# Attention values and output projection of a vision tower: Wv and Wo multiplied into one matrix, or applied one after the other

## The reference, cut to what matters

```python
# _L0_ffn_ref: x is (64, 170, 128); 2 heads of 64
hx = _layernorm(x, ln_g, ln_b)
q = (hx @ Wq).reshape(b, n, h, dh).transpose(0, 2, 1, 3)
k = (hx @ Wk).reshape(b, n, h, dh).transpose(0, 2, 1, 3)
v = (hx @ Wv).reshape(b, n, h, dh).transpose(0, 2, 1, 3)
...                                  # q, k normalised, causal scores, softmax
o = jnp.einsum('bhqk,bhkd->bhqd', attn, v)
y = o.transpose(0, 2, 1, 3).reshape(b, n, d) @ Wo
gate = jax.nn.softmax(y @ gate_W + gate_b, axis=-1)
hid = jax.nn.gelu(jnp.einsum('bnd,edf->bnef', y, W1) + b1)   # 8 experts, all of them
eo = jnp.einsum('bnef,efd->bned', hid, W2) + b2
out = jnp.einsum('bned,bne->bnd', eo, gate)
```

## Time and profile before

| | us |
|---|---|
| time, median of 3 (1700.39 to 1704.64) | 1700.49 |
| the profiled execution's own time | 1700.59 |
| its span, first to last instruction | 1698.5 |
| TensorE busy | 1569.1 |
| VectorE busy | 1304.2 |
| ScalarE busy | 1090.9 |
| GpSimd busy | 370.5 |

### The profile page before, as it was taken

One profiled execution on the slowest core, in us unless ns is written; L12 is line 12 of the kernel. 1 busy time (PEld: TensorE's weight loads), 2 busy tenths in 40 slices (PEclk: granted clock), 3 DMA queues, 4 the chain that ended last, 5 costly groups with the idle time before them and its releaser, 6 DMA issues.

```text
span 1698.5 us, 31246 instructions
## 1 busy us (share of the span) xinstructions
PE 1569.1 (92%) x10875; PEld 1105.7 (65%) x10875; DVE 1304.2 (77%) x2462; ACT 1090.9 (64%) x1833; POOL 370.5 (22%) x213
## 2 busy tenths in 40 slices
PE   6984599999999999999999999999999999999988
PEld 3542476667676676666676767666676767677665
DVE  7993378696878778796878777786968787777766
ACT  2321267676776767676767767676767677676766
POOL 5456002021211202020212112020202121120313
PEclk8996599999998989899999989899999999898979
DMA  4311010010101010100101010102001010101020
GB/s 179 130 44 72 0 67 1 26 49 8 66 8 66 8 66 0 74 0 19 55 8 66 8 66 8 66 0 74 0 15 60 8 66 8 66 8 67 1 75 9
DMA packets 14255, 68.88 MB, mean 41 GB/s; under 512 B 1808, under 2 KB 1808, under 8 KB 11664
## 3 DMA queue, kind: packets, MB, share of 16 engines
q1 hardware_dynamic: 13936, 67.71, 11.0%
q10 hardware_dynamic: 288, 0.77, 0.1%
HBM read 62.56 MB, written 5.92 MB: 40 GB/s over the span
## 4 chain that ended last, share of the span: by engine, by line
PE 79%; DVE 13%; issue 4%; ACT 3%; DMA 0%; POOL 0%; DVEq 0%; POOLq 0%; ACTq 0%
PE pair L864 23%; PE pair L881 23%; PE pair L667 8%; PE pair L808 4%; PE pair L653 4%; PE pair L679 2%; PE pair L751 2%; PE pair L766 2%; PE pair L695 2%; DVE root_t L1051 2%; PE pair L781 2%; PE pair L796 2%; DVE area L1131 2%; DVE root_t L1053 1%; PE pair L848 1%
## 5 line engine op out<-in xcount | busy, mean ns | idle before, releaser
L1208 DVE TENSOR_TENSOR area<-area 128x680 f16<-128x680 f32 x512 | 529.2, 1038 | 89.3 <-ACT area L566 80.5
L561 ACT ACTIVATE area<-pair,pack_b_sb 128x680 f32<-128x680 f32 x512 | 425.9, 832 | 237.8 <-PE pair L864 235.3
L864 PE MATMUL pair<-area,ws 128*128 128x340 f16 x3072 | 562.7, 322 | 0.2 <-ACT area L566 0.2
L881 PE MATMUL pair<-area,ws 128*128 128x340 f16 x3072 | 534.0, 310 | 13.0 <-DVE area L1220 12.3
L864 PEld LDWEIGHTS pair<-area,ws 128*128 128x128 f16 x3072 | 310.4, 102 | 162.6 <-ACT area L566 3.6
L881 PEld LDWEIGHTS pair<-area,ws 128*128 128x128 f16 x3072 | 296.8, 98 | 160.3 <-DVE area L1220 20.3
L399 POOL TENSOR_TENSOR area<-area 128x680 f32<-128x680 f32 x112 | 215.7, 1926 | 642.9 <-DVE area L1220 642.9
L566 ACT ACTIVATE area<-pair,pack_b_sb 128x680 f16<-128x680 f32 x384 | 317.8, 828 | 0.0
L1220 DVE SCALAR_TENSOR_TENSOR area<-pair,pack_b_sb,area 128x340 f32<-128x340 f32 x256 | 134.4, 565 | 40.9 <-PE pair L881 40.9
L396 POOL TENSOR_TENSOR area<-area,ht 128x680 f32<-128x680 f32 x16 | 33.7, 2107 | 589.9 <-DVE area L1220 589.9
L531 ACT ACTIVATE area<-pair,nbias,root 85x85 f32<-85x85 f32 (+1 forms) x256 | 112.3, 463 | 17.3 <-DVE nbias L1119 17.3
(11 more groups left out here) (180 smaller groups left out, 1780.9 us busy)
## 6 DMA issues: line engine op xcount, KB each, us to landing
area<-gate_scratch SPq DMA_DIRECT2D x16, 1360.0 KB, 9.9
area<-gate_scratch SPq DMA_DIRECT2D x16, 1020.0 KB, 7.1
area<-cells SPq DMA_DIRECT2D x14, 448.0 KB, 3.5
area<-gate_scratch SPq DMA_DIRECT2D x16, 340.0 KB, 4.4
tower_out<-area SPq DMA_DIRECT2D x16, 340.0 KB, 2.3
area<-cells SPq DMA_DIRECT2D x13, 416.0 KB, 4.1
area<-w SPq DMA_DIRECT2D x1, 2048.0 KB, 9.9
pack_b_sb<-pack_b SPq DMA_DIRECT2D x1, 1044.0 KB, 9.8
```

The lines of the kernel that those rows point to most:

```text
L561: nc.scalar.activation(two(hid[slot % NHID]), halves(hid_ps[slot % 2]), ACT.Gelu_apprx_tanh, bias=col(COL_B1 + slot)).then_inc(hid_ready, 1)
L864: last = mm(hid_ps[slot % 2][:, j, 0:TH], lhs[:, w], rhs[:, j * TH:(j + 1) * TH], start=(i == 0), stop=(i == 2))
L881: last = mm(eo_ps[:, j, 0:TH], lhs[:, w], rhs[:, j * TH:(j + 1) * TH], start=(m % CH == 0 and i == 0), stop=(m % CH == CH - 1 and i == 2))
L1208: v.tensor_tensor(hl[slot % NPART], hid[slot % NHID], hh[slot % NPART], ALU.subtract).then_inc(hlo_ready, 1)
```

## The change

Wv and Wo are not multiplied with each other any more.
- Preparation: the products and copies for `wvo` are gone. VectorE splits `wv` (128 x 128) into `wv_h`, `wv_l`. The bias column comes from one product with `wv`.
- `values`: the moving operand is `wv_h` or `wv_l` with 128 columns; `values_evac` copies 256 columns an image in place of 512.
- `weigh`: the weights of a head are its 85 x 64 values, and the result goes to its 64 partitions of PSUM (and of the array's columns), so the heads no longer add up into the same place.
- New on ScalarE: `o_evac(j)` copies half j of the weighted values, with the bias, to `o32` (in the place of `qs`). New on TensorE: `project(j)`, one f32 product of `wo` with that half, 340 columns, into `hid_ps[1]`. `y_evac(j)` now waits for it, and copies from there without a bias.
- Order: TensorE has `project(0)` between `weigh(2)` and `weigh(3)`, `project(1)` between `var2` and the logits. ScalarE has `o_evac(0)`, `y_evac(0)`, sq2, `o_evac(1)`, `y_evac(1)`, the variance's evacuation. VectorE has dev2 ahead of `y_parts(0)`.

```diff
-        wqk_h, wqk_l, wvo_h, wvo_l = (sb(n, [128, 2 * D], F16) for n in ("wqk_h", "wqk_l", "wvo_h", "wvo_l"))
+        wqk_h, wqk_l = (sb(n, [128, 2 * D], F16) for n in ("wqk_h", "wqk_l"))
+        wv_h, wv_l = (sb(n, [128, D], F16) for n in ("wv_h", "wv_l"))
...
-                nc.scalar.activation(vp[:, b * 512:(b + 1) * 512], hid_ps[b // 2][0:QC, b % 2, :],
+                nc.scalar.activation(vp[:, b * 2 * D:(b + 1) * 2 * D], hid_ps[b // 2][0:QC, b % 2, 0:2 * D],
                                      ACT.Copy).then_inc(vp_ready, 1)
...
+            def o_evac(g, j):
+
+                act.wait_ge(pv_ps, NB * g + 2 * (j + 1))
+                nc.scalar.activation(o32[:, j * TH:(j + 1) * TH], hid_ps[0][:, j, 0:TH], ACT.Identity,
+                                     bias=att_b[:, 2:3]).then_inc(o_ready, 1)
+
             def y_evac(g, j):
 
-                act.wait_ge(pv_ps, NB * g + 2 * (j + 1))
-                nc.scalar.activation(y32[:, j * TH:(j + 1) * TH], hid_ps[0][:, j, 0:TH], ACT.Identity,
-                                     bias=att_b[:, 2:3]).then_inc(y_ready, 1)
+                act.wait_ge(y_ps, 2 * g + j + 1)
+                nc.scalar.activation(y32[:, j * TH:(j + 1) * TH], hid_ps[1][:, j, 0:TH], ACT.Copy).then_inc(y_ready, 1)
...
+                o_evac(g, 0)
                 y_evac(g, 0)
                 if ahead:
                     graph(g + 1, "sq2")
+                o_evac(g, 1)
                 y_evac(g, 1)
...
-                    for h in range(H):
-                        last = mm(hid_ps[h][:, 1, 0:D], wv_t[h * DH:(h + 1) * DH, :],
-                                  wo_s[h * DH:(h + 1) * DH, :], start=True, stop=True)
...
-                    for h in range(H):
-                        last = mm(hid_ps[0][:, 0, 2 * D + 2:2 * D + 3], wvo[:, h * D:(h + 1) * D], col(COL_LNB),
-                                  start=(h == 0), stop=(h == H - 1))
-                    last.then_inc(pe_prep, 1)
+                    mm(hid_ps[0][:, 0, 2 * D + 2:2 * D + 3], wv_s, col(COL_LNB), start=True, stop=True).then_inc(pe_prep, 1)
...
-                    for n, (x_part, w_part) in enumerate(((xh_h, wvo_h), (xh_l, wvo_h), (xh_h, wvo_l))):
-                        last = mm(hid_ps[b // 2][0:QC, b % 2, k * H * D:(k + 1) * H * D],
+                    for n, (x_part, w_part) in enumerate(((xh_h, wv_h), (xh_l, wv_h), (xh_h, wv_l))):
+                        last = mm(hid_ps[b // 2][0:QC, b % 2, k * D:(k + 1) * D],
                                   x_part[:, t * QC:(t + 1) * QC], w_part[:, :], start=(n == 0), stop=(n == 2))
...
-                        v0 = b * 512 + k * H * D + h * D
+                        v0 = b * 2 * D + k * D + h * DH
...
-                        last = mm(hid_ps[0][:, b // 2, y0 + k * QC:y0 + TOK], vp[:, v0:v0 + D],
-                                  pt[b % 2][0:QC, p0:p0 + TOK - k * QC],
-                                  start=(k == 0 and h == 0), stop=(k == 1 and h == H - 1))
+                        last = mm(hid_ps[0][h * DH:(h + 1) * DH, b // 2, y0 + k * QC:y0 + TOK], vp[:, v0:v0 + DH],
+                                  pt[b % 2][0:QC, p0:p0 + TOK - k * QC], start=(k == 0), stop=(k == 1))
                 last.then_inc(pv_ps, 1)
+
+            def project(g, j):
+
+                pe.wait_ge(o_ready, 2 * g + j + 1)
+                mm(hid_ps[1][:, j, 0:TH], wo_s, o32[:, j * TH:(j + 1) * TH], start=True, stop=True).then_inc(y_ps, 1)
...
                 weigh(g, 2)
+                project(g, 0)
                 weigh(g, 3)
                 graph_of("var2")
+                project(g, 1)
...
-                y_parts(g, 0)
                 if ahead:
                     graph(g + 1, "dev2")
+                y_parts(g, 0)
                 y_parts(g, 1)
```

More of the change, by code:

```diff
@@ L75 @@
 PACK_A = {"gamma": SHIFTS * NP * NP, "conv_w": SHIFTS * D}
-PACK_B = {"beta": SHIFTS * NP * NP, "cols": 39, "scal": 28, "wp": 5 * D, "wv_t": D, "wo": D,
+PACK_B = {"beta": SHIFTS * NP * NP, "cols": 39, "scal": 28, "wp": 5 * D, "wv": D, "wo": D,
           "wqk": 2 * D, "gate_w": E, "gate_b": E, "b2": E}
@@ L115, in vit_tower @@
         gam, conv_w, beta, cols, scal = (packs[n] for n in ("gamma", "conv_w", "beta", "cols", "scal"))
-        wp_t, wv_t, wo_s, wqk_s = (packs[n] for n in ("wp", "wv_t", "wo", "wqk"))
+        wp_t, wv_s, wo_s, wqk_s = (packs[n] for n in ("wp", "wv", "wo", "wqk"))
         gate_ws, gate_bs, b2_s = packs["gate_w"], packs["gate_b"][0:QC, :], packs["b2"]
@@ L137, in vit_tower @@
         gcn_c = sb("gcn_c", [128, 1])
-        wvo = sb("wvo", [128, H * D])
-        wqk_h, wqk_l, wvo_h, wvo_l = (sb(n, [128, 2 * D], F16) for n in ("wqk_h", "wqk_l", "wvo_h", "wvo_l"))
+        wqk_h, wqk_l = (sb(n, [128, 2 * D], F16) for n in ("wqk_h", "wqk_l"))
+        wv_h, wv_l = (sb(n, [128, D], F16) for n in ("wv_h", "wv_l"))
         att_b = sb("att_b", [128, 4])
@@ L196, in vit_tower @@
         gbc = take(E * T)
-        vp = gbc[0:QC, 0:NB * 512]
-        probs = gbc[0:QC, NB * 512:NB * (512 + 6 * QC)]
-        assert NB * (512 + 6 * QC) <= (E - 1) * T
+        o32 = qs
+        vp = gbc[0:QC, 0:NB * 2 * D]
+        probs = gbc[0:QC, NB * 2 * D:NB * (2 * D + 6 * QC)]
+        assert NB * (2 * D + 6 * QC) <= (E - 1) * T
         tmp = [take(T) for _ in range(2)]
@@ L233, in vit_tower @@
         nb_ready, exp_ready, rs_ready, p_ready = map(sem, ("nb_ready", "exp_ready", "rs_ready", "p_ready"))
-        pt_ps, pt_ready, pv_ps, y_ready = map(sem, ("pt_ps", "pt_ready", "pv_ps", "y_ready"))
+        pt_ps, pt_ready, pv_ps, o_ready = map(sem, ("pt_ps", "pt_ready", "pv_ps", "o_ready"))
+        y_ps, y_ready = map(sem, ("y_ps", "y_ready"))
         yh_ready, yl_ready = map(sem, ("yh_ready", "yl_ready"))
@@ L241, in vit_tower @@
         half_used, half_ready, out_done = map(sem, ("half_used", "half_ready", "out_done"))
-        PREP_PE, PREP_ACT, PREP_DVE = 8, 9, 22
+        PREP_PE, PREP_ACT, PREP_DVE = 8, 7, 22
         def col(n):
@@ L430, in prep_evac @@
                                          bias=col(COL_BP)).then_inc(act_prep, 1)
-                    nc.scalar.activation(wvo[:, 0:D], hid_ps[0][:, 1, 0:D], ACT.Copy).then_inc(act_prep, 1)
-                    nc.scalar.activation(wvo[:, D:2 * D], hid_ps[1][:, 1, 0:D], ACT.Copy).then_inc(act_prep, 1)
                 if p == 6:
@@ L630, in prepare @@
                     for k in range(4):
-                        mm(hid_ps[0][:, 0, D:D + 1], wp_t[:, (k + 1) * D:(k + 2) * D], scal[:, 24 + k:25 + k],
-                           start=(k == 0), stop=(k == 3))
-                    for h in range(H):
-                        last = mm(hid_ps[h][:, 1, 0:D], wv_t[h * DH:(h + 1) * DH, :],
-                                  wo_s[h * DH:(h + 1) * DH, :], start=True, stop=True)
+                        last = mm(hid_ps[0][:, 0, D:D + 1], wp_t[:, (k + 1) * D:(k + 2) * D], scal[:, 24 + k:25 + k],
+                                  start=(k == 0), stop=(k == 3))
                     last.then_inc(pe_prep, 1)
                 if p == 5:
-                    pe.wait_ge(act_prep, 7)
+                    pe.wait_ge(act_prep, 5)
                     mm(hid_ps[0][:, 0, 2 * D:2 * D + 1], wqk_s[:, 0:D], col(COL_LNB), start=True, stop=True)
                     mm(hid_ps[0][:, 0, 2 * D + 1:2 * D + 2], wqk_s[:, D:2 * D], col(COL_LNB), start=True, stop=True).then_inc(pe_prep, 1)
-                    for h in range(H):
-                        last = mm(hid_ps[0][:, 0, 2 * D + 2:2 * D + 3], wvo[:, h * D:(h + 1) * D], col(COL_LNB),
-                                  start=(h == 0), stop=(h == H - 1))
-                    last.then_inc(pe_prep, 1)
+                    mm(hid_ps[0][:, 0, 2 * D + 2:2 * D + 3], wv_s, col(COL_LNB), start=True, stop=True).then_inc(pe_prep, 1)
             def conv(p):
@@ L964, in prepare @@
                                 v.scalar_tensor_tensor(dst, src, w, dst, ALU.mult, ALU.add).then_inc(dve_prep, 1)
-                    dve.wait_ge(act_prep, 7)
                     for n, (src, hi, lo) in enumerate((
-                            (wqk_s, wqk_h, wqk_l), (wvo[:, :], wvo_h, wvo_l), (adj_t[:, :], adj_h, adj_l),
+                            (wqk_s, wqk_h, wqk_l), (wv_s, wv_h, wv_l), (adj_t[:, :], adj_h, adj_l),
                             (wp_t[:, 0:D], plain_h, plain_l))):
@@ L1296 @@
         "wp": a("L0_attn_Wp").reshape(D, D, 5).transpose(1, 2, 0).reshape(D, -1),
-        "wv_t": a("L0_ffn_Wv").T, "wo": a("L0_ffn_Wo"), "wqk": np.concatenate([a("L0_ffn_Wq"), a("L0_ffn_Wk")], axis=1),
+        "wv": a("L0_ffn_Wv"), "wo": a("L0_ffn_Wo"), "wqk": np.concatenate([a("L0_ffn_Wq"), a("L0_ffn_Wk")], axis=1),
         "gate_w": a("L0_ffn_gate_W"), "gate_b": np.tile(a("L0_ffn_gate_b"), (128, 1)),
```

## The result

The changed kernel takes 1727.55 us (median of four runs, 1726.13 to 1728.91), the kernel before, measured beside it, 1702.15 (1700.39 to 1704.64). The ratio is 1.0144, with a 95% interval of 1.0125 to 1.0163: slower, as forecast (1714), but by some 25 us instead of 13, and 2.5 us above the range. The profiled execution took 1728.91 us with a span of 1726.8, 28.3 more than the span of before.

What follows compares the result with a forecast made beforehand. TensorE's stream and its breaks bound the kernel; delaying the logits' end delays the group. From 1700.59 us: groups 14 x 0.2 = 2.8, clock 15 x 0.8 = 12, ends +0.8, -1.8, -0.3, sum +13.5: 1714; range 1701 to 1725.

Steps and rivals of the forecast that it cites:

- Part 1: Value products of 128 columns: 0.33 us each instead of 0.65, gaining 1.05 us a group up to the scores.
- Part 2: Weighings in half the array's columns: heads side by side, 0.52 us instead of 0.99 to 1.02.
- rival of serial halves: Weighing: the two heads' halves run one after the other, 0.89 us, +0.67 us a group, 1724; chance 0.16.
- the scores' ratio: Scores take 1.05 us against 1.77 in series, 0.59 of it; applied to the weighing, this gave 0.52 us.
- Part 3: Projection and evacuations: waits for h2 and the square, attention 1.25 us longer; net of values +0.2 us a group.
- The three distances: Starts of weigh(0) to weigh(2), weigh(2) to variance, variance to logits; the forecast's timeline put them at 3.55, 2.44, 2.61 us.
- Part 4: Clock around variance, projection and logits: it falls earlier against the logits, costing 0.8 us a group.
- Its rule: Clock falls stay 1.9 to 4.4 us after dense work ends, so 1.0 to 3.5 us after the variance's new start.
- rival of no clock price: Before the cast, the change costs nothing through the clock: 1702 us; chance 0.21.
- rival of a faster kernel: Low-clock stretch has its own length, so beginning earlier it ends earlier after the cast: 1691 us; chance 0.08.
- The ends: Outside the middle groups: first group +0.8 us, last group -1.8 us, preparation -0.3 us.
- Preparation: Before the groups: six short f32 passes fewer, -0.3 us (0 to -0.46).

Runs made afterwards that it cites:

- e7: Kernel before with only value products of 128 columns and evacuations of 256, both heads weighing the first head's values: 1689.29 us, ratio 0.9921.
- e9: Changed kernel with four dense unread products in TensorE's wait before the variance: 1707.37 us, ratio to before 1.0033.
- e10: Changed kernel with four dense unread products in TensorE's wait before the logits: 1729.63 us, ratio to before 1.0153.
- e4: Changed kernel with ScalarE's square put ahead of y_evac(0): 1701.57 us, ratio to before 0.9989.
- e6: Kernel before with twelve dense unread products in the middle of each group's expert work (slot 24): 1731.74 us, ratio 1.0177.
- the last pair: Both with 14 dense products before the cast and sums cut; changed kernel, also square first and four before logits, 1665.17 us; kernel before 1679.58.
- e8: Changed kernel with the weighing's loops over heads and key halves exchanged: 1728.94 us, ratio to before 1.0159.
- e2: Changed kernel with dense unread products: four before the variance, four before the logits, 14 before the cast: 1680.06 us, ratio to before 0.9867.

## Why the prediction was right, and where it was wrong

**Part 1** right: 0.33 us a product by the rate of the earlier trace rows, 1.04 us a group for a forecast of 1.05, and e7 shows 11.6 us of it in the time. Even the wait of 0.23 us for the low half is there. The value product before this experts_out began at 784.36 and took 0.33, so TensorE was free at 784.69; the low half (L1214) ended at 784.86:

```profile
784.92 1.04 PE L888 MATMUL pair<-area,ws 128*128 128x340 f16 x6
```

```profile
782.84 2.02 DVE L1214 TENSOR_TENSOR area<-area 128x680 f16<-128x680 f32 x1 [0.42 <-ACT area L573]
```

The Trainium skill ("TensorE: Matmul & The Clock Gate", Back-to-back issue gap) has about 81 ns for a sustained pair of weight load and 128-column matmul. Here six of them in 0.33 us are 56 ns each, and the measurement decides.

**Part 2** right, though not by its reason. The rival of serial halves is out (0.59, not 0.89). The halves run side by side. At 145 and 72 ns a pass that would be 145 + 145 + 72 + 72 ns = 0.43 us; some 0.16 come on top, 0.05 in the first step (195 ns) and 0.11 between the last pair and the turn (0.18 us for 0.07). The change of tiling is the likely cause. It would also lie behind the turn after a weighing, 0.61 us where it was 0.46, and mean2 with 1.23 where four such passes took 1.18. The prediction took 0.52 from the scores' ratio and let the price of a change of tiling be inside it; what stands next to a weighing pays too. The Trainium skill ("TensorEngine Tiling (Array Packing)", Key Properties) names a drain at a change of tiling mode. The trace agrees as far as it goes: pieces on either side of a weighing are 0.05 to 0.2 us longer, but no run varies the tiling alone.

**Part 3** right in its mechanism, short in its size. The waits for ScalarE are where they were put: TensorE is idle for 0.61 us before the variance (0.8 forecast), since the square, behind y_evac(0), starts 0.85 us after dev2's end (0.7 forecast), and for 0.62 before the logits (0.65). Only the 0.25 us of waiting for h2 don't show: the weighings and turns ahead of mean2 had grown by more than that. The three distances were 3.64, 2.63 and 2.68 us for 3.55, 2.44 and 2.61, and the turns 0.09 more: projection(0) took 0.78 instead of 0.59, and the longer pieces beside weighings come on top. Net of part 1 a group costs 0.54 instead of 0.2. Of these 0.34, 0.06 are a slip of the sum (794.66 less 793.35 is 1.31, not 1.25), 0.09 the turns, 0.19 what lies between weigh(0) and the logits. Over 14 groups that is 5 of the 14.8 us that the forecast missed.

**Part 4** had the right mechanism and the wrong size: 0.8 us a group forecast, 1.12 measured, 4.5 us over 14 groups. Its rule moved the falls to 1.0 to 3.5 us after the start of the variance, and the price worked out from them was about 1.1; they came at 0.9 to 3.1 (3.7 in the first group), and the price is what was measured. The step that failed is the one after it, 0.8 for falls spread evenly over the gap. The falls of after did spread over the gap, but a spread is not so cheap: a fall anywhere ahead of the logits costs all of their 1.23 us. From 1.0 to 3.5 us, 1.6 of 2.5 lie ahead of the logits (2.6 to 3.85), which alone is 0.8 us. By the prediction's own terms, as an estimate, falls inside the logits add 0.3, those inside the variance and projection 0.2, and what the logits of before lose comes off: about 1.2. That 1.1 and 1.12 agree so closely is in part luck, since the 1.1 was worked out for two clusters and "logits at 2.4 in about half of the groups", and they are low in every one but the first (2.46 us from logits to reader in the mean). Together the two terms, part 3's 0.2 for 0.54 and part 4's 0.8 for 1.12, are why the time lies above the range.

What makes the falls come when they do, the prediction had only in part: it moved them 0.9 us for the earlier end of the dense work. e9 and e10 show more: the hole before the variance, followed by thin passes, brings the early fall. With only that hole filled the grants from the variance's start are 0.77 to 1.00, falls at 2.8 us or later, and logits to reader takes 1.53 us (2.46 in after, 1.56 in before) at the same waits; filling the later hole alone does nothing. e4 shows the same by an order of two instructions. The other part is the place of the logits: by e6, falls nearly as early cost little where the logits begin 1.23 us after the variance. So the rival of no clock price was not far off for the projection itself: with the hole filled (e9) or gone (e4, 1.74 us) the dense projection between variance and logits leaves the clock nearly as it was before. The rival of a faster kernel had a little for it: over 7 us from the cast the grant is 0.70, where the same group had 0.65 in the earlier trace rows, so 4.2 us of low clock behind the cast instead of 4.9, and cast to sums is 0.30 us shorter (18.29, 18.59). But half-clock time from 200 us to the end of the span rose from 177 to 237 us.

```profile
812.42:819.42 7.00, 7.00 (x42) 5.01 (x43) 3.99 (x6) 3.53 (x6) 0.00 (x0) 0.70 0.02 3
```

**The ends.** The first group's 1.4 us more than forecast are clock too: it falls inside the scores and the graph work. Rows of the chain of after, first group, where the last piece before the scores' second round takes 3.69 us and 2.02 in a later one (788.96):

```profile
215.91 3.69 PE pair L668 x10
219.60 1.05 PE pair L782 x16
```

Why just there isn't known; no run was made on it. The last group gives +0.37 where -0.5 was forecast. It was at half clock in both kernels, and the projection's two halves and a wait for ScalarE stand where they were put:

```profile
1655.21 1.43 PE pair L816 x2
1656.64 1.07 PE pair L809 x8
...
1657.74 0.55 ACT area L539
...
1658.33 1.51 PE pair L816 x2
```

They answer to the earlier trace rows. The weighings take 1.05 and 1.07, together the 2.1 of the forecast; each half of the projection takes 1.43 to 1.51 where 1.18 was put, which is 0.6 us, and a turn behind a weighing takes 1.09 instead of 0.86, 0.46 for the two. The forecast had a slip here too: its terms from the scores on (3.99 to 2.1 and 1.18, 1.9 saved, 2.1 for 0.65) add up to -1.2, not to the -0.5 that its -1.8 leaves without the values. Preparation: the 2.6 us between forecast and profile are within what the same code does from one profile to the next.

So of 14.8 us missed, 4.8 are waits and lengths, 4.5 the clock and 0.7 the stretch behind the cast in 14 groups, 4.0 the preparation and the first group, 0.9 the last.

What stays open: why the grants of e9 and e4 take turns between groups, and what of the dear logits of before (1.56 against 1.41) could be had without dense products.

## What to carry to other kernels

When a change puts an instruction into a queue, look for who stands behind it: here one evacuation ahead of a square made 0.6 us of silence on TensorE just before thin passes, and that cost 26 us in 1728, only 10 of them as waiting. Where TensorE must wait next to thin work, the wait itself can be the smaller part of the price; move it, or fill it with products that compute nothing, and measure which of several holes matters, since here only one of two did. A comparison of two kernels whose clocks differ says little on the arithmetic: with dense products in the holes these two took the same time, though their groups at full clock were 0.55 us apart, and in the last pair only 2 of 14 us were not clock. Compare groups that ran at full clock from end to end.

## What the runs showed of the hardware that was not expected

- Passes for the two halves of the array's columns run side by side even if all those of one half are issued first (0.60 us for eight passes in e8, 0.59 in after). The Trainium skill ("TensorE: Matmul & The Clock Gate", Part 3: Packing small matmuls — row/col tiling, The mechanism) has matmuls start and end in strict order; for halves of the columns the records of e8 don't agree.
- Pieces beside half-column passes are 0.05 to 0.2 us longer (a turn 0.61 for 0.46, mean2 1.23 for 1.18, half a projection 0.78 for 0.59).
- Thin passes double at half clock like others do: 16 logits passes 1.23 us and 2.47.
- Four products of 0.6 us that compute nothing, in one place, are worth 20 us (e9), and 22 products a group 47 (e2).
